# An image table with four offset rows innermost, gathered as runs of 1023 words

## The reference

```
xp = c * gx - s * gy + dx0;   yp = s * gx + c * gy + dx1      # per image: angle, shift
ix = (yp / h * 2 + 1) * 0.5 * (w - 1);   iy = (xp / w * 2 + 1) * 0.5 * (h - 1)
out = sum over the four neighbours of X[iy + a, ix + b] * weight(a, b)
x = warp(x, side, angle);  x = attention(x);  x = reaction(x);  x = experts(x)
```

## Time and profile before

| | |
|---|---|
| median of 3 runs | 945.78 us (945.24 to 951.15) |
| profiled execution | 950.23 us, of which the span of its instructions is 948.4 us |
| PE busy | 703.7 us (74%) |
| DVE busy | 471.5 us (50%) |
| ACT busy | 359.9 us (38%) |
| POOL busy | 312.0 us (33%) |
| queue of SP's and ACT's transfers | 150.78 MB, 48.1% of the 16 engines' span |
| queue of POOL's transfers | 61.51 MB, 20.9% |

### The profile page before, as it was taken

The page is one execution under the profiler, slowest core; times in us unless marked ns, Lnnn a source line. Parts: engine busy times, 40 slices in busy tenths (PEclk is TensorE's granted clock), DMA queues, the critical chain, the costliest instruction groups (busy, mean ns, idle before and its releaser), DMA issues.

```text
span 948.4 us, 14765 instructions
## 1 busy us (share of the span) xinstructions
PE 703.7 (74%) x4659; PEld 488.7 (52%) x4659; DVE 471.5 (50%) x1013; ACT 359.9 (38%) x912; POOL 312.0 (33%) x292
## 2 busy tenths in 40 slices
PE   0441222365678888988899998899869999999992
PEld 0341111142234343534345542788759999989881
DVE  6435555597575776475777774446411221211210
ACT  0121333254367754446364557312203233222320
POOL 1103454485698842200110006302622112111112
PEclk9866555586599999989999999899989999999997
DMA  6999888689763303996911003767879999899961
GB/s 216 301 270 313 279 285 284 226 281 329 206 240 118 113 2 115 282 333 226 368 73 47 1 2 124 264 232 220 291 228 331 316 328 329 280 354 379 342 165 22
DMA packets 136208, 216.17 MB, mean 228 GB/s; under 512 B 10357, under 2 KB 102058, under 8 KB 135978
## 3 DMA queue, kind: packets, MB, share of 16 engines
q1 hardware_dynamic: 114808, 150.78, 48.1%
q0 software_dynamic: 16784, 61.51, 20.9%
q10 hardware_dynamic: 4546, 3.08, 1.1%
HBM read 160.87 MB, written 56.37 MB: 229 GB/s over the span
## 4 chain that ended last, share of the span: by engine, by line
DMA 34%; PE 29%; DVE 17%; issue 8%; POOL 7%; ACT 2%; SPq 1%; DVEq 1%; POOLq 1%; ACTq 0%
DMA results<-arena,home 13%; DMA result<-arena,home 7%; DVE arena L1730 7%; PE psum L1433 5%; PE psum L1262 5%; DMA table<-arena 4%; PE psum L1447 3%; PE psum L1495 3%; PE psum L1504 3%; DMA arena<-table,tap_col 3%; POOL pairs_x L1018 2%; DMA arena<-qk_rows 2%; POOL arena L883 2%; PE psum L1396 2%; PE psum L1275 2%
## 5 line engine op out<-in xcount | busy, mean ns | idle before, releaser
L1182 ACT ACTIVATE arena<-psum 128x512 f32<-128x512 f32 (+3 forms) x384 | 170.5, 492 | 133.5 <-PE psum L1452 95.8
L1730 DVE TENSOR_REDUCE arena<-psum 128x2 f32<-128x1024 f32 (+2 forms) x192 | 176.2, 954 | 64.7 <-PE psum L1268 50.6
L1232 ACT ACTIVATE arena<-psum,b_cols 128x128 f32<-128x128 f32 x312 | 84.7, 382 | 234.8 <-PE psum L1495 234.8
L1495 PE MATMUL psum<-arena 128*128 128x128 f32 x1248 | 150.5, 280 | 6.5 <-issue 3.6
L1495 PEld LDWEIGHTS psum<-arena 128*128 128x128 f32 x1248 | 149.1, 197 | 9.7 <-issue 8.1
L1504 PE MATMUL psum<-arena 128*128 128x256 f32 x624 | 143.5, 384 | 10.7 <-DVE arena L2062 10.7
L1262 PE MATMUL psum<-arena 96*128 96x512 bf16 (+3 forms) x384 | 109.7, 352 | 32.4 <-DMA arena<-qk_rows 16.9
L1504 PEld LDWEIGHTS psum<-arena 128*128 128x128 f32 x624 | 116.9, 192 | 26.7 <-issue 12.0
L1447 PE MATMUL psum<-arena 99*128 99x512 bf16 (+3 forms) x384 | 113.8, 334 | 13.9 <-ACT arena L1182 8.2
L2058 DVE TENSOR_TENSOR arena<-psum,arena 128x256 f32<-128x256 f32 x39 | 16.6, 424 | 159.6 <-PE psum L1504 85.5
L1262 PEld LDWEIGHTS psum<-arena 96*128 96x128 bf16 x384 | 35.3, 102 | 105.0 <-DVE arena L1730 52.8
(11 more groups left out here) (212 smaller groups left out, 907.6 us busy)
## 6 DMA issues: line engine op xcount, KB each, us to landing
arena<-L_ffn_W SPq DMA_DIRECT2D x78, 1024.0 KB, 7.4
pairs_x<-zeros SPq DMA_DIRECT2D x4, 4160.0 KB, 25.5
arena<-qk_rows SPq DMA_DIRECT2D x16, 768.0 KB, 11.2
table<-arena SPq DMA_DIRECT2D x20, 384.0 KB, 9.6
qk_rows<-arena SPq DMA_DIRECT2D x16, 384.0 KB, 5.4
arena<-pairs_x SPq DMA_DIRECT2D x39, 130.0 KB, 6.5
qk_rows<-arena SPq DMA_DIRECT2D x16, 256.0 KB, 5.7
padded<-arena SPq DMA_DIRECT2D x2, 1328.0 KB
```

The source lines that it names most:

```text
L1182: nc.scalar.activation(probs[at % 2][h][:, q0:512], banks[turn % SCORE_BANKS][:, q0:512], ACT.Exp, scale=DH ** -0.5).then_inc(exp_done, 1)
L1232: ins = nc.scalar.activation(hidden_t[k % SLOTS][:, f], banks[hidden_bank(k) + f // 4][:, (f % 4) * P:(f % 4 + 1) * P], ACT.Relu, bias=b1_ ...
L1495: ins = t_.matmul(banks[first + f // 4][:, (f % 4) * P:(f % 4 + 1) * P], w1_slot[u][:, c, f * P:(f + 1) * P], x_t[:, c], start=c == 0, sto ...
L1730: return v.reduce_max(part[:, 2 * pair:2 * pair + 2, qb], psum[:, first:first + 2, 0:keys], AX_X)
```

## The change

The table gets two ranges (NW) of four offset rows (RW) in place of six rows: range 0 has rows 0 to 3, range 1 rows 2 to 5. The row is the innermost index: a word lies at column x range x sheared column x row, so 640 x 4 words a range (WINDOW). Three neighbouring rows lie in one of the ranges, and a block's taps of one column are one run of 256 x 4 - 1 = 1023 words (TAP_RUN). The index arithmetic of `rows_of` picks the range. The table has 5120 words a column for 3840.

The strip tile is [3, 2, 128, 4]: a copy out of PSUM now writes three rows with a step of four words, and one more copy of 128 elements per group writes the row that both ranges hold. SP stores it in runs of 512 words. In the taps, element j of row r lies at 4j + r, so that DVE's and POOL's operations on taps step by four words. The blocks' results and hats stay contiguous.

Image 1's blocks get other places. Blocks 0 and 1 use the free part of x1, the area "mix" and the place of stack 3 (kind 0); the blocks after them use x1, mix and the part of the turned image (xwT) that held image 0. So there are four sets of semaphores for three, gather 3 and the hats of block 2 wait until image 0's values are out (`v_ready`), gather 3 no longer waits for stored parts, and SP waits before it loads stack 3 until blocks 0 and 1 are mixed and the transpose of block 0 has been copied.

```diff
@@ -30,8 +30,11 @@
-RUNS = [(0, 2 * J + D)]
-LANDED = 16 * (1 + 3 * len(RUNS))
+NW, RW = 2, 4
+WINDOW = J * RW
+TAP_WORDS = D * RW
+TAP_RUN = TAP_WORDS - 1
+LANDED = 16 * (1 + 3)
@@ -78,7 +81,8 @@
-MIX_AT, MIX_HATS = 24984, 24984 + 2 * 3 * 2 * 256
+MIX_AT = 24984
+SPARE_AT = (NG - 1) * HG * S
@@ -191,14 +195,14 @@
-        table = [dram(f"table{b}", [XW * R * J]) for b in range(NB)]
+        table = [dram(f"table{b}", [XW * NW * WINDOW]) for b in range(NB)]
...
-        table_v = [t.rearrange("(x r j) -> x r j", x=XW, r=R) for t in table]
+        table_v = [t.rearrange("(x w n) -> x w n", x=XW, w=NW) for t in table]
@@ -278,18 +282,17 @@
-        strip = [tile([3, R, P]) for u in range(2)]
-        tap_words = [tile([9 * J - (J - D)]) for u in range(2)]
-        taps = []
-        for u in range(2):
-            at = 2 * BAND + 2 * 3 * R * P + u * (9 * J - (J - D))
-            taps.append(arena[:, at:at + 9 * J].rearrange("p (d r j) -> p d r j", d=3, r=3)[:, :, :, 0:D])
-        pad_rows = [region(2 * BAND + 2 * 3 * R * P + b * SB * PADW)([SB, PADW]) for b in range(NB)]
+        strip = [tile([3, NW, P, RW]) for u in range(2)]
+        pad_rows = [region(2 * BAND + 2 * 3 * NW * RW * P + b * SB * PADW)([SB, PADW]) for b in range(NB)]
+        tap_words = [tile([3, TAP_WORDS]) for u in range(2)]
+        taps = [words.rearrange("p d (j r) -> p d r j", r=RW)[:, :, 0:3] for words in tap_words]
...
-        slow = [(tile([5, D]), tile([D, 2]), tile([D], I32), tile([8]), tile([1], I32), tile([PADW + 2]))] * 2
+        slow_rows = tile([5, D])
+        slow = [([slow_rows[:, i] for i in range(5)], tile([D, 2]), tile([D], I32), tile([8]), tile([1], I32),
+                 tile([PADW + 2]))] * 2
@@ -316,37 +319,42 @@
-        def column(words, at):
-            return words[:, at:at + 3 * J].rearrange("p (r j) -> p r j", r=3)[:, :, 0:D]
-        late_places = [[(x1_words, 0), (x1_words, 2 * J + D), (arena, MIX_AT)],
-                       [(arena, MIX_AT + 2 * J + D), (arena, late_at), (arena, late_at + 2 * J + D)],
-                       [(arena, MIX_AT + 2 * J + D), (arena, PROBS_AT), (arena, PROBS_AT + 2 * J + D)]]
-        late_taps = [[column(*place) for place in places] for places in late_places]
-        late_words = [[words[:, at:at + 2 * J + D] for words, at in places] for places in late_places]
-        late_x1 = x1_words[:, 2 * (2 * J + D):]
-        tile = region(late_at + 2 * (2 * J + D))
-        late_hats = [[late_x1[:, 0:3 * D].rearrange("p (k d) -> p k d", k=3), region(MIX_HATS)([3, D])],
-                     [tile([3, D]), tile([3, D])],
-                     [region(PROBS_AT + 2 * (2 * J + D))([3, D]), region(O_GROUP_AT)([3, D])]]
+        xw_left = [warped_words[:, c * NB * S:c * NB * S + S] for c in range(DC)]
+        mix = arena[:, MIX_AT:MIX_AT + 2 * TAP_WORDS + 2 * 3 * D + 2 * D]
+        spare = arena[:, SPARE_AT:SPARE_AT + HG * S // 2]
+        def piece(words, at, n):
+            return words[:, at:at + n]
+        first_taps = [piece(x1_words, d * TAP_WORDS, TAP_WORDS) for d in range(3)]
+        second_taps = [piece(mix, d * TAP_WORDS, TAP_WORDS) for d in range(2)]
+        first_hat, second_hat = piece(x1_words, 3 * TAP_WORDS, 3 * D), piece(mix, 2 * TAP_WORDS, 3 * D)
+        second_other = piece(mix, 2 * TAP_WORDS + 3 * D, 3 * D)
+        late_words = [first_taps, second_taps + [piece(xw_left[1], 0, TAP_WORDS)],
+                      first_taps, second_taps + [piece(spare, TAP_WORDS, TAP_WORDS)]]
+        late_taps = [[words.rearrange("p (j r) -> p r j", r=RW)[:, 0:3] for words in columns] for columns in late_words]
+        hat_words = [[first_hat, piece(xw_left[0], 0, 3 * D)], [second_hat, second_other],
+                     [first_hat, piece(spare, 0, 3 * D)], [second_hat, second_other]]
+        late_hats = [[words.rearrange("p (k d) -> p k d", k=3) for words in both] for both in hat_words]
...
-        late_frac = [sb("late_frac", [P, D, 2])[:], tile([D, 2]), region(V_GROUP_AT)([D, 2])]
-        late_warped = [late_x1[:, 3 * D:4 * D], tile([D]), region(MIX_HATS + 3 * D)([D])]
+        first_frac = sb("late_frac", [P, D, 2])[:]
+        second_frac = piece(mix, 2 * TAP_WORDS + 2 * 3 * D, 2 * D).rearrange("p (d t) -> p d t", t=2)
+        late_frac = [first_frac, second_frac, first_frac, second_frac]
+        second_warped = piece(x1_words, 3 * TAP_WORDS + 3 * D, D)
+        late_warped = [piece(xw_left[0], 3 * D, D), second_warped, piece(spare, 3 * D, D), second_warped]
...
-        for u in range(3):
-            first, second, third = late_words[u]
-            late_slow.append((third[:, 0:5 * D].rearrange("p (k d) -> p k d", k=5), late_frac[u],
-                              second[:, D:2 * D].bitcast(I32), second[:, J + D:J + D + 8],
-                              second[:, J + D + 8:J + D + 9].bitcast(I32), first[:, D:D + PADW + 2]))
+        for u in range(4):
+            wide, other = hat_words[u]
+            late_slow.append(([piece(late_words[u][2], i * D, D) for i in range(4)] + [piece(wide, D, D)], late_frac[u],
+                              piece(wide, 0, D).bitcast(I32), piece(other, 0, 8), piece(other, 8, 1).bitcast(I32),
+                              piece(other, D, PADW + 2)))
...
-            return 2 if k == 1 else k % 2
+            return 2 + k if k < 2 else k % 2
...
-            return 1 if k < 2 else k // 2 + 1 - k % 2
+            return 1 if k < 2 else k // 2
@@ -396,8 +404,8 @@
-        late_frac_in = [sem(f"late_frac_in{u}") for u in range(3)]
-        late_taps_in = [sem(f"late_taps_in{u}") for u in range(3)]
+        late_frac_in = [sem(f"late_frac_in{u}") for u in range(4)]
+        late_taps_in = [sem(f"late_taps_in{u}") for u in range(4)]
@@ -651,8 +659,8 @@
-                        sp.dma_start(table_v[b][x0:x0 + w, :, bass.ds(q * P, P)],
-                                     strip[u][0:w, k]).then_inc(strip_stored[u], 16)
+                        sp.dma_start(table_v[b][x0:x0 + w, :, bass.ds(q * (P * RW), P * RW)],
+                                     strip[u][0:w, k].rearrange("p w q r -> p w (q r)")).then_inc(strip_stored[u], 16)
@@ -680,6 +688,9 @@
+                if g == NG - 1:
+                    sp.wait_ge(late_mixed, 2)
+                    sp.wait_ge(max_read, USE_OF["turn_w", 0, 1] + 1 + 2)
@@ -786,7 +797,7 @@
-            us, vs, fl, ab, ix = (slow[:, i] for i in range(5))
+            us, vs, fl, ab, ix = slow
@@ -878,12 +889,10 @@
-                                for r, words in RUNS:
-                                    at_ = (d * 3 + r) * J
-                                    nc.gpsimd.indirect_dma_start(
-                                        tap_words[u][:, at_:at_ + words], None, table[b].unsqueeze(0),
-                                        bass.IndirectOffsetOnAxis(ap=tap_col[:, u:u + 1], axis=1),
-                                        element_offset=(d * R + r) * J).then_inc(taps_landed[u], 16)
+                                nc.gpsimd.indirect_dma_start(
+                                    tap_words[u][:, d, 0:TAP_RUN], None, table[b].unsqueeze(0),
+                                    bass.IndirectOffsetOnAxis(ap=tap_col[:, u:u + 1], axis=1),
+                                    element_offset=d * NW * WINDOW).then_inc(taps_landed[u], 16)
@@ -918,26 +927,24 @@
-                    for slot in range(PART_SLOTS):
-                        pool.wait_ge(parts_stored[slot], PART_STORES * 2)
+                    pool.wait_ge(v_ready, 1)
...
-                    g_.indirect_dma_start(late_words[u][d], None, table[1].unsqueeze(0),
+                    g_.indirect_dma_start(piece(late_words[u][d], 0, TAP_RUN), None, table[1].unsqueeze(0),
...
-                                          element_offset=d * R * J).then_inc(late_taps_in[u], 16)
+                                          element_offset=d * NW * WINDOW).then_inc(late_taps_in[u], 16)
...
-                if k == 1:
+                if k < 2:
...
-                if k == 3:
-                    for slot in range(PART_SLOTS):
-                        pool_hold(parts_stored[slot], PART_STORES * 2)
+                if k in (2, 3):
+                    pool_hold(v_ready, 1)
@@ -1081,8 +1088,8 @@
-                    if k == 1:
-                        act.wait_ge(xwT_done, SB + 2)
+                    if k == 2:
+                        act.wait_ge(v_ready, 1)
@@ -1102,8 +1109,10 @@
-                        nc.scalar.activation(strip[u][0:w, k, 3 * half:3 * half + 3],
-                                             banks[g][0:w, 0:3 * P].rearrange("p (r q) -> p r q", r=3),
+                        nc.scalar.activation(strip[u][0:w, k, half, :, half:half + 3].rearrange("p q r -> p r q"),
+                                             banks[g][0:w, 0:3 * P].rearrange("p (r q) -> p r q", r=3), ACT.Copy)
+                        at_ = 0 if half else 2 * P
+                        nc.scalar.activation(strip[u][0:w, k, 1 - half, :, 3 * half], banks[g][0:w, at_:at_ + P],
```

(17 more changed lines are left out.)

## The result

The changed kernel takes 993.21 us (986.07 to 993.76, four runs) beside 945.99 us for the kernel before (945.24 to 951.15, four runs): ratio 1.046, 95% interval 1.0423 to 1.0497. The profiled execution of after has a span of 991.9 us, 43.5 more than before's 948.4. The forecast was 981, in a range of 936 to 1014.

The account below looks back on a forecast made before the run. Bounds taken: transfers and a table store for strips, gathers, hats and DVE mixing in turn for pairs, then PE with 2.2 us of slack to POOL. Strips 3 + pairs 12 + POOL 20.4 = +35.4: 981 us, range 936 to 1014.

Parts of the forecast that it names:

- The step that priced DVE: Image 0's mixing on DVE: 0.63 ns more per element, charged once whatever operands are strided; +3.2 us a block.
- the head sum: A DVE sum reading SBUF at 68 bytes: 272 elements in 614 ns against 443 contiguous, giving 0.63 ns an element.
- Strip: Turning and storing image 0's strips: strided copies, extra small copies and larger stores, +3 us, of 0 to 13.
- Ring: A pair of image 0's blocks, gather through hats to mixing: 24.4 us before, 27.5 after; +12 in four pairs.
- The landing: Wait from a block's last gather to its taps: 5.5 us, cut by 1.2 to 4.3, bounds 0.8 and 1.8.
- Projection: From 182 to 222 us: smaller gathers save 0 to 5.2 us, swallowed because POOL sets the pace.
- POOL: Image 1's sums beside the attention: +4.5 us a block, last block 20.4 us past when PE wants it.
- 0.63 per strided input: Image 1's operations on POOL: 0.63 ns per element for each strided input, products +0.48 us, sums of 768 +0.97.
- Edits at nothing: Address arithmetic, the wait before loading stack 3, and the new wait of gather 3 and block 2's hats: no cost.
- no stride costs anything: Rival, chance 0.20: 16-byte steps are free; -2.9 us a pair, -12 in four, projection -5; 929 us.
- Only one engine pays: Rival, chance 0.14: strides slow only DVE, 956 us, or only POOL, 957 us.
- two readings of the note on cachelines: Strided tap accesses: either moving to a new 16-byte line costs, as the forecast took, or four fp32 go free.

Follow-up runs that it names:

- the section on the strip copies: Changed kernel with DVE's and POOL's products and sums row innermost, and ACT's and DVE's strip copies also written row innermost: 946.49 us, ratio 0.9999.
- the bytes alone: Kernel before, old table and contiguous operations, each gather of taps fetching 1023 words instead of 1536, so warp's values differ: 941.92 us, ratio 0.9928.
- POOL in the other order: Changed kernel with POOL's products and sums of 768 row innermost: 965.39 us; with DVE's product and sums of 768 row innermost as well: 948.34 us.
- DVE alone paying: Changed kernel with only POOL's three products and two sums of 768 a block walking the same words row innermost: 965.39 us, ratio 1.0178.
- POOL alone: Changed kernel with only DVE's product of 2304 and two sums of 768 walking the same words row innermost: 976.06 us, ratio 1.0281.

## Why the prediction was right, and where it was off

The forecast was slower by the strides, on both engines, and that is what happened; the runs show it rather than argue it, since the order alone takes the loss of products and sums away on either engine. The total came out below what was measured, 35.4 us for 43.5 in the profiles, and partly by errors that cancel. The step that priced DVE was right in kind: one surcharge per element, whatever the number of strided operands (product, sums and row product have two or three). The size was 0.63 ns an element from the head sum of the earlier trace rows and came out as 0.74 for the product ((4254 - 2558) / 2304) and 0.77 for the sums.

Term by term:

- **Strip, +3 forecast, +4.0 measured.** The stride cost 0.40 us a copy on ACT (894 for 491 ns) and 0.28 on DVE (828 for 548), where 0.24 each had been put down. The 4.0 compares one profile with one: as the section on the strip copies shows, the end of this stage varies by some 2 us from profile to profile, and the order of the copies takes back about 2, which leaves nothing that can be told for the larger stores.
- **Ring, 27.5 forecast, 29.8 measured.** DVE's block was 10.2 and not 9.65: 1.1 us on two blocks. The last gather ended 0.83 and not 0.35 us behind DVE: 0.5. The landing took 5.06 and not 4.3: the smaller gathers gave back 0.4 us here and 0.85 in the kernel with the bytes alone, not 1.2. Together these are the 2.3. The forecast also set out from a ring of 24.4 for all pairs; before's starts are 23.8, 25.4 and 25.0 apart. Four pairs: 12 forecast, 18.9 measured, the largest miss. By the table, the three distances between starts grew by 5.7, 4.4 and 4.6, the last pair took 5.4 more up to the projection, and the first one's taps came 1.2 sooner.
- **Projection, a gain of 0 to 5.2 forecast and called swallowed, 3.8 lost.** The step that failed is the reading of the earlier trace rows there: DMA at 0.89 was taken for what the stage could win. DMA fell to 0.68, and the stage got longer, because DVE's operations wait while POOL multiplies and adds. Before's casts have a mean of 1093 ns for the 1339 of after:

```profile
L1719 DVE CAST arena<-arena 128x512 bf16<-128x512 f32 x8 | 8.7, 1093 | 0.0
```

  On the timeline of after, one cast runs beside a product of POOL, one behind the last sum of its block, and a DVE operation on two elements lasts from 236.71 to 243.39, through three of POOL's products (236.91 to 243.37):

```profile
217.67 2.65 POOL L966 TENSOR_TENSOR x<-x 128x768 f32<-128x768 f32 x1
218.19 2.42 DVE L1728 CAST arena<-arena 128x512 bf16<-128x512 f32 x1
...
231.85 0.42 DVE L1728 CAST arena<-arena 128x512 bf16<-128x512 f32 x1
...
236.71 6.68 DVE L1792 TENSOR_SCALAR z_cols<-z_cols 128x2 f32<-128x2 f32 x1
```

  Beside POOL's first late block, four casts and three products of DVE each end 0.27 to 0.54 us after an operation of POOL does. Against before, the casts take 2.0 us more in all, these products 2.0 and the operation on two elements 1.1; of these 5.1 us 3.8 are left at the first maximum. POOL's longer operations made the waits longer; the kernels with POOL in the other order took them back. Nothing of the forecast named DVE as waiting for POOL.
- **POOL, 4.5 us a block forecast and 20.4 in all; 4.0 a block and 18.2 measured.** Near in sum and wrong in parts. "0.63 per strided input" made the product 2.29 (2.20 measured), the column sum 2.78 (3.09) and the sums of 256 1.04 (0.64). That the sum came near is luck: the errors cancel. What counts is how many places the operands open: the column sums open them in two columns, the row sums in one, which both operands share.
- **Edits at nothing.** SP's wait ahead of stack 3 cost nothing that shows, and the wait ahead of gather 3 (8.16 us in the earlier trace rows) is gone: after's POOL issues gather 3 from 255.09, behind two copies for v and without a wait. Neither mattered to the end.

The sum: 4.0 + 18.9 + 3.8 + 18.2 = 44.9, of which 1.4 came back. The forecast's 35.4 lacked 1.0 on the strip, 6.9 on the pairs and 3.8 in the projection, and had 2.2 too much on POOL.

Of the rivals, "no stride costs anything" has its nearest kernel in the bytes alone, which gave 941.9, not 929: 5.6 us up to the projection and 2.1 in it, where 12 and 5 had been credited. Its mechanism needs an order in which the strides don't cost, and its size was too large. "Only one engine pays" was wrong in price as well as in fact: with DVE alone paying the kernel was 965, with POOL alone 976, not 956 and 957. With DVE alone, strips and pairs cost 22.9 us and not 15, and the projection gave back 1.4 and not 5. With POOL alone, strips and loop were to win 9 us and lost 2.3 (the projection started at 184.44 for 182.10), and POOL's order held up DVE in the projection for 1.8 us more.

The forecast weighed two readings of the note on cachelines in the Trainium skill's "SBUF — State Buffer". Its rule that a 16-byte line wants two accesses for full bandwidth agrees with DVE at a step of two words (2559 ns, no surcharge) and of three and four (3257, 4254). It doesn't agree with POOL, which pays at two words as well (2205 against 1808); nor do these rows agree there with the Trainium skill's "GPSIMD Engine Reference", section "Performance pitfalls for Q7 kernels", whose surcharge begins above 8 bytes. The 6.0 us a block that the forecast estimated by that page was further from the measured 4.0 than its own 4.5. The last words of the note on cachelines, that four fp32 go free, agree with neither engine: four words is where every element opens a line, and where both pay most.

## What to carry to other kernels

Look at an access pattern by how many 16-byte places each operand opens, not by whether the layout is interleaved: the same words in the order in which they lie side by side took back a 4.6% loss as far as it can be told, without a byte moved. Before counting a byte saving as time, find the wait that it shortens, here 0.4 to 0.85 us of a ring of 24. And when an engine off the path gets slower, ask who else waits while it works.

## What the runs showed of the hardware

- DVE: a place of 16 bytes costs 1.85 to 2.06 ns on operations of 768 and 2304 words, a word about 1.1 to 1.25; the longer total shows. Both hold a fixed part: from 768 to 2304, a word adds 1.04 ns (958 to 2558) and a place 1.76 (1548 to 4254). Further strided operands add nothing (1512 ns for the row product with two, 1548 for the sums with three), and neither does a step of 32 bytes (618 for 610). ACT's strip copies show the same kind of surcharge: 894 for 491 ns when each of 384 words goes to a place of its own.
- POOL: the time rises with the places of all inputs together, some 1.1 ns each in the column sums, from the first step on; two operands in the same places are cheap (0.64 us for 256 words, 1.09 to 1.18 in different places). Two rows aren't on that line and stay open. The sum in the same places takes less than the contiguous one (0.64 for 0.72), though its operands open 256 places for 128. And before's contiguous products of 768 words took 1.81 us, the row-innermost one, which opens fewer places because its weight repeats, 1.59, and after's, with 960 places, 2.20.
- A DVE cast of 0.42 us took 2.4 to 3.3 us in after, and 2.0 in before, while POOL's products and sums ran, and ended 0.27 to 0.29 us after one of them; an operation on two elements waited 6.7 us, through three products that followed on each other. The terms of the Trainium skill's "SBUF — State Buffer" say that DVE and GpSimd contend for a port pair that is held for a whole instruction; the casts agree with it.
